# Deformable convolution, main loop: the second odd spread moved behind the first tap's matmuls of a step

## The reference, cut to what matters

```python
om = conv3x3(x, w_off) + b_off
off_y, off_x, mask = om[:, :9], om[:, 9:18], sigmoid(om[:, 18:])
py = off_y + row + ky
px = off_x + column + kx
sampled = bilinear(x, py, px) * mask
out = einsum('bckhw,ock->bohw', sampled, w) + b
return relu(batch_norm(out)) + x
```

## Time and profile before

| | |
|---|---|
| median of 3 runs | 2130.82 us (2126.55 to 2131.65) |
| the profiled execution's own time | 2128.34 us |
| its span | 2126.5 us |
| busy of the span | PE 75%, PEld 51%, DVE 76%, ACT 68%, POOL 30% |
| main loop, by the trace | from 565 to 1894 us of the span |

### The profile page before, as it was taken

The page is one execution under the profiler, slowest core; times in us unless marked ns, Lnnn a source line. Parts: engine busy times, 40 slices in busy tenths (PEclk is TensorE's granted clock), DMA queues, the critical chain, the costliest instruction groups (busy, mean ns, idle before and its releaser), DMA issues. The chain is left out here.

```text
span 2126.5 us, 63487 instructions
## 1 busy us (share of the span) xinstructions
PE 1587.5 (75%) x24974; PEld 1087.2 (51%) x24975; DVE 1622.4 (76%) x2176; ACT 1443.3 (68%) x2225; POOL 636.1 (30%) x1200
## 2 busy tenths in 40 slices
PE   4767453120399999999999999999999999961710
PEld 3644221010276666666766766666666667640310
DVE  5344587495599999999989999999999999962205
ACT  1211226245499999999999999999999999950102
POOL 3000111100234444434444444444444344410000
PEclk9679776665599999999999999999999999995555
DMA  3075368777757776676676676776776777730008
GB/s 127 0 198 140 87 230 282 204 271 255 234 133 165 164 159 159 155 160 158 159 169 149 158 164 155 158 172 162 159 155 154 161 163 159 161 55 4 0 4 368
DMA packets 291492, 333.27 MB, mean 157 GB/s; under 512 B 73736, under 2 KB 265609, under 8 KB 289163
## 3 DMA queue, kind: packets, MB, share of 16 engines
q1 hardware_dynamic: 240550, 260.38, 46.1%
q0 software_dynamic: 48128, 67.28, 14.1%
q10 hardware_dynamic: 2534, 1.72, 0.4%
HBM read 230.42 MB, written 98.63 MB: 155 GB/s over the span
## 5 line engine op out<-in xcount | busy, mean ns | idle before, releaser
L152 POOL DMA_DIRECT2D rows<-scratch_parts x1152 | 588.4, 519 | 730.2 <-PE ps_even_y L764 707.5
L914 DVE TENSOR_TENSOR G<-odd_y,ps_odd_v 128x504 f32<-128x504 f32 (+2 forms) x928 | 571.7, 658 | 93.7 <-PE ps_odd_v L794 58.6
L794 PE MATMUL ps_odd_v<-tent_x,stage 32*128 32x171 f32 (+1 forms) x5568 | 636.2, 323 | 0.0
L860 ACT COPY odd_y<-ps_odd_y 128x504 f32<-128x504 f32 (+2 forms) x928 | 526.6, 567 | 62.2 <-PE ps_odd_y L773 24.7
L773 PE MATMUL ps_odd_y<-rows,sel 32*128 32x504 f32 (+2 forms) x928 | 459.7, 495 | 119.0 <-ACT sel L842 105.0
L794 PE MATMUL ps_even_v<-tent_x,stage 32*128 32x171 f32 (+3 forms) x5568 | 534.2, 322 | 13.1 <-ACT even_v L866 12.7
L923 DVE TENSOR_TENSOR G<-even_v,ps_even_y 128x1008 f32<-128x1008 f32 (+2 forms) x464 | 538.9, 1161 | 1.2 <-ACT even_v L866 0.9
L794 PEld LDWEIGHTS ps_odd_v<-tent_x,stage 32*128 32x128 f32 x5568 | 507.9, 186 | 0.0
L794 PEld LDWEIGHTS ps_even_v<-tent_x,stage 32*128 32x128 f32 x5568 | 420.5, 186 | 155.6 <-issue 150.5
L812 PE MATMUL ps_r<-G,conv_w 128*32 128x224 f32 (+1 forms) x8832 | 475.9, 342 | 0.7 <-ACT res L871 0.7
L866 ACT COPY even_v<-ps_even_v 128x1008 f32<-128x1008 f32 (+2 forms) x464 | 451.0, 972 | 19.5 <-PE ps_odd_v L794 9.6
(11 more groups left out here) (134 smaller groups left out, 960.1 us busy)
## 6 DMA issues: line engine op xcount, KB each, us to landing
place<-scratch_om SPq DMA_DIRECT2D x960, 105.0 KB, 3.5
rows<-scratch_parts POOLq DMA_DIRECT2D x960, 52.5 KB, 3.6
scratch_parts<-high SPq DMA_DIRECT2D x16, 1764.0 KB
scratch_parts<-tent_y SPq DMA_DIRECT2D x16, 1764.0 KB
place<-scratch_om SPq DMA_DIRECT2D x192, 84.0 KB, 2.7
scratch_om<-om SPq DMA_DIRECT2D x64, 165.4 KB
rows<-scratch_parts POOLq DMA_DIRECT2D x192, 42.0 KB, 2.8
scratch_conv<-res SPq DMA_DIRECT2D x448, 14.0 KB, 2.0
```

The lines of the kernel that those rows point to most:

```text
L152: eng.dma_start(bass.AP(tensor=rows[b][:].tensor, offset=32 * g * pitch + here, ap=[[2 * pitch, Y_KINDS], [GROUP * W, 3], [1, count * W]]) ...
L794: m = nc.tensor.matmul(sub(ps_v[g // 2], 0, 128, i * 512 + lo + first, dims), stage[32 * g:32 * g + 32, j * IMAGE + v * C:j * IMAGE + (v + ...
L860: nc.scalar.copy(odd_y[p % 3][:, i * ROW + lo:i * ROW + hi], ps_odd_y[:, lo:hi]).then_inc(odd_kept, 1)
L914: nc.vector.tensor_tensor(sub(G, 0, 128, slot(v) + i * ROW + lo, [[1, hi - lo]]), odd_y[p % 3][:, i * ROW + lo:i * ROW + hi], ps_v[1][:, i ...
```

## The change

In `reduce` an optional argument `to` is new. Where a step has a quarter of a convolution, the second odd spread is no longer issued ahead of it but inside it, behind the matmuls of its first tap (k = 2t). Where a step has none (p = 4, and the first four steps), it stays where it was. With it goes its wait for `odd_kept`. The order within `sample` is untouched, as are all other engines' lists.

```diff
-                def reduce(it, blk, t):
+                def reduce(it, blk, t, to=None):
...
                         if k == KK - 1:
                             m.then_inc(reduced, 1)
+                        if k == 2 * t and to:
+                            spread_odd(*to, 1)
...
                         sample(it, p, to)
                         spread_even(it, p)
-                        if to:
-                            spread_odd(*to, 1)
                         if at := block_of(it, p):
                             if at[2] == 0:
                                 pe.wait_ge(even_weighted, STEPS * at[0] + BLOCK // 2 * (at[1] + 1) + 1)
-                            reduce(*at)
+                            reduce(*at, to)
+                        elif to:
+                            spread_odd(*to, 1)
```

## The result

The changed kernel takes **2170.7 us** (median of 4 runs, 2167.0 to 2172.6) against 2131.2 of the kernel before (also 4 runs; the 2130.8 above is of three of them): ratio 1.0184, 95% interval 1.016 to 1.0209. The forecast was 2173, slower. Its profiled execution took 2171.2 us with a span of 2169.4, which is 42.9 longer than the one before.

A forecast was written before the change was run, and what follows sets the result against it. TensorE was fullest, the odd spread held by ScalarE's copy, VectorE a near second. Shape changes around the moved spread add 0.38 us a block, 111 blocks, +42 us: 2128.3 to 2170.5, plus 2.5 for the median, 2173; range 2135 to 2205.

The forecast's parts named there:

- What bounds the step: Main loop, changed kernel: first tap starts at the larger of +1.31 and even spread + 0.42; step is that + 1.46.
- The inserted piece, 0.56: Moved odd spread between two taps on TensorE: 0.14 + 0.42 = 0.56 us with both shape changes.
- the account: The prediction's step-by-step timing of TensorE in the main loop: +0.38 us a block, 111 blocks, +42 us.
- The bound below, 0.28: Least time of the moved spread between taps, if shape changes were free: 0.28 us.
- The step lengths: Steps p = 9 to 12 of a pair: 2.77, 2.98, 2.83, 3.30 us, sum 11.88 against 11.50.
- The second clock: VectorE's even product lets the following even spread begin only 3.87 or 3.93 us after a step's sample.
- The same price at a pair's seams: Blocks at a pair's seams, with narrower views and one step without taps, were taken to cost +0.38 us too.
- s: Start of the even spread within a step: 3.87 (3.93 from the second step) less the length of the step before.
- Rival B: Between the taps only the uncovered weight load is paid, piece 0.38 us: break-even, +2 us, 2133; chance 0.09.
- C: ScalarE wait was the bound, shape changes free, piece 0.28 us: faster, -20 us, 2111; chance 0.09.
- D: Each half of the convolution pays 0.10 us more for loads: 44 us more, 2217; chance 0.10.
- wait of 84 us: Odd spread's weight load waiting for ScalarE's copy, 347 times, 84.1 us; forecast to disappear, only part to be had.

The follow-up runs named there:

- the small matmul: Kernel before plus a 32-row, 8-column matmul behind the first tap of every quarter, order kept: 2277.5 us, ratio 1.0677.
- the halved product: Changed kernel with VectorE's even product made for one image of the pair only, from the second pair on: 2125.6 us, ratio 0.9976.

## Why the prediction was right

- **What bounds the step** held. Start of the first tap = the larger of +1.31 and even spread + 0.42: measured +1.31 in p = 9, and 1283.44 less 1283.01, 0.43, in p = 10.
- **The inserted piece, 0.56**: measured in the first step as 1281.90 less 1280.45, 1.45 for two taps and all; the account had 1.46. The bound below, 0.28 with free changes of shape, is refuted by the changed kernel and by the small matmul, which alone costs 0.32 with 8 columns.
- **The step lengths** forecast as 2.77, 2.98, 2.83 and 3.30 came as 2.76, 2.99, 2.83 and 3.31; +0.38 a block forecast, +0.39 measured. 111 blocks of 0.39 are 43.3, and the span grew by 42.9.
- **The second clock** through VectorE's even product, which turns a cost of nothing into one of 0.2 in the step p = 10, is shown by the halved product: 45 us, as expected.
- **The total** agrees better than its parts, and that is luck. Ordinary pairs grew from 82.6 to 85.4 us, +2.8, where the account has 7 blocks of 0.38, 2.7. The same price at a pair's seams was only assumed: p = 5 pays 0.36 (3.23 against 2.87), which the account's own rule gives if the short step ahead of it is put in (s = 3.93 - 2.58 = 1.35). The first pair grew from 88.2 to 93.9, 5.7 instead of 2.3, its steps p = 5, 6 and 7 taking 4.93, 4.93 and 4.25 against 4.40, 3.35 and 2.78. And a few pairs of the kernel before were longer than 82.6, the longest 84.0, by some 4 us in all, those of the changed kernel hardly ever longer than 85.4, which takes the surplus back.
- **Rival B** (only one uncovered load, no change in time) and **C** (free changes, faster) fall with the measured 0.51 and 0.43. **D** (0.10 more) isn't seen. The **wait of 84 us** did go, but most of it could not be had: with it gone the first tap still has to let the even spread through (0.43), and the spread's old place was the one where it needs no further change of shape.
- **One sign was read wrongly in advance**: I said the wait for ScalarE's copy would be gone from the waits view. The view still has 61.3 us of it, 172 times. The timeline shows moved spreads that start 0.4 us or more behind the copy's end (0.63 in p = 10; 0.26 in p = 0), and those of p = 4, not moved, 0.05 behind it. The idle time of the others stands where the shape changes, and the view names the last semaphore it saw. In the same way it names ScalarE as what VectorE's odd product waits for (61.6 us), though that product still starts (1286.34) within 0.01 of ScalarE's even copy, which waits for the sample.
- The Trainium skill, TensorEngine Tiling (Array Packing), section Tiling Modes, says that changing the mode, not just the tile, drains TensorE. The runs agree in what it costs: 0.32 us a step for the mode, nothing measurable for another tile. That the cost is a drain they don't show. The estimate of 53 ns a change from the Trainium skill, TensorE: Matmul & The Clock Gate, section What happens when you issue a matmul, is a third of what 0.32 for two comes to.
- Still only argued: the share of a drain in that 0.32. Not tested: whether the type of the spread (float32r between float32 taps) has a share in it.

## What to carry to other kernels

Before a small matmul is moved into another group to hide a wait, look at the shapes (rows and output columns) on both sides of its old and new place: here giving up a wait of 0.2 us a step bought two changes of shape at 0.33. Then follow the next-latest wait: a second clock held the first tap at +1.54, +1.38 and +1.48 in three steps of four, where the array would have allowed +1.31, and all of the loss in an ordinary block came through it. A resource with one buffer sets not only who waits but who is queued behind the waiter.

## What the runs showed of the hardware that I had not expected

A float32r matmul that keeps the taps' 128 rows and changes their output columns (128 x 128 between 128 x 32) costs as much as one that changes the rows, 0.33 against 0.32 us a pair; it also changes the type, so the columns are not shown to be the cause. The kernel that makes half of VectorE's even products had the same time as the kernel before (2129.7 against 2132.3): an engine with 92% busy time in the loop gave nothing back when each of these products fell from 1.20 to 0.67 us. The account had forecast that, but the busy share by itself would not let one guess it.
